# Joint last stage: PSUM dealt out as two banks for jobs and two for the turned probabilities, instead of three and one

## What is computed

```python
xn = layernorm(x)
qkv = xn @ w_qkv.T                       # 16 heads of 16 columns
q, k = rmsnorm(q) * q_norm_w, rmsnorm(k) * k_norm_w
p = softmax(q @ k.T * 16 ** -0.5)        # per sequence and head, 256 x 256
s = (p @ v) @ w_proj.T + b_proj
# 8 experts of width 176, two of them kept per token, and a shared expert of 352
g = sum_e c[e] * (silu(xn @ gate[e]) * (xn @ up[e]) @ down[e]) + shared(xn)
x = x + s * silu(g)
```

## Time and profile before

| | |
|---|---|
| median of 3 runs | 1460.88 us (1456.83 to 1460.98) |
| the profiled execution: device time | 1457.64 us |
| its span | 1455.8 us |
| mean granted clock of TensorE | 0.98 |
| PE busy over the span | 1374.6 us, 94% |
| DVE, ACT, POOL busy | 63%, 56%, 53% |
| the last stage | from 909.5 us to the end, 546 us |

### The profile page before, as it was taken

How to read it: one execution, slowest core, us unless ns; L and a number is a source line. 1 busy time by engine, 2 the same in 40 slices (tenths; PEclk the granted TensorE clock), 3 DMA queues, 4 the chain that set the end, 5 groups by cost and what they waited for, 6 DMA issues and landing times. The chain is left out here.

```text
span 1455.8 us, 25701 instructions
## 1 busy us (share of the span) xinstructions
PE 1374.6 (94%) x8880; PEld 1231.8 (85%) x8880; DVE 917.8 (63%) x1781; ACT 822.4 (56%) x2172; POOL 764.7 (53%) x759
## 2 busy tenths in 40 slices
PE   6988799999999999999999997889999999999997
PEld 5877689998899989998899986678888888889896
DVE  5554565665656565666656664676777777776654
ACT  4543454445444554445554443367777687777773
POOL 1642243445344454435455434577669667766764
PEclk9999999999999999999999999899999999999999
DMA  5877333234331343323433423234233232342442
GB/s 171 292 265 263 82 93 99 74 83 115 111 87 48 106 123 100 89 52 102 124 87 79 118 80 130 78 122 128 81 103 118 85 118 90 107 131 85 127 132 72
DMA packets 85681, 165.64 MB, mean 114 GB/s; under 512 B 16720, under 2 KB 27664, under 8 KB 83248
## 3 DMA queue, kind: packets, MB, share of 16 engines
q1 hardware_dynamic: 85552, 163.99, 37.2%
HBM read 99.90 MB, written 22.09 MB: 84 GB/s over the span
## 5 line engine op out<-in xcount | busy, mean ns | idle before, releaser
L750 POOL TENSOR_TENSOR a_pr<-a_pr,a_ri 128x512 f32<-128x512 f32 x128 | 133.2, 1041 | 304.7 <-DVE a_ri L930 304.5
L807 ACT ACTIVATE a_pr<-a_score,a_nb 128x256 f32<-128x256 f32 x256 | 118.9, 469 | 270.2 <-DVE a_nb L922 270.2
L1277 POOL TENSOR_TENSOR l_pr<-l_pr,l_ri 128x512 f32<-128x512 f32 x128 | 133.2, 1041 | 136.5 <-DVE l_ri L1647 135.3
L1405 ACT ACTIVATE l_pr<-l_score,l_nb 128x256 f32<-128x256 f32 x256 | 119.1, 471 | 84.1 <-DVE l_nb L1618 83.4
L55 PE MATMUL a_job<-s_xs,s_wh 128*128 128x512 f32 x384 | 156.1, 407 | 5.1 <-PEq L204 5.1
L56 PE MATMUL a_job<-s_xs,s_wh 128*128 128x512 f32 x384 | 152.6, 397 | 0.0
L57 PE MATMUL a_job<-s_xs,s_wl 128*128 128x512 f32 x384 | 151.9, 396 | 0.0
L922 DVE TENSOR_REDUCE a_nb<-a_score 128x2 f32<-128x512 f32 x128 | 88.4, 691 | 89.7 <-PE a_score L993 89.4
L1618 DVE TENSOR_REDUCE l_nb<-l_score 128x2 f32<-128x512 f32 x128 | 87.4, 683 | 29.4 <-PE l_score L1743 29.1
L935 DVE TENSOR_TENSOR a_pt<-a_turn,a_pt 128x512 fp32r<-128x512 f32 x128 | 87.4, 683 | 24.4 <-ACT a_pt L815 24.4
L1767 PE MATMUL l_out<-s_wh,l_vp 128*128 128x256 f32 x512 | 93.1, 304 | 0.9 <-DVE s_wh L1622 0.9
(11 more groups left out here) (239 smaller groups left out, 4811.5 us busy)
## 6 DMA issues: line engine op xcount, KB each, us to landing
s_wl<-wgu_scratch SPq DMA_DIRECT2D x56, 512.0 KB, 4.7
a_sk<-a_rotk SPq DMA_DIRECT2D x384, 64.0 KB, 2.0
a_sq<-a_rotq SPq DMA_DIRECT2D x256, 64.0 KB, 2.0
s_xs<-xn_scratch SPq DMA_DIRECT2D x14, 1024.0 KB, 5.7
l_wd<-wd_scratch SPq DMA_DIRECT2D x56, 256.0 KB, 2.7
a_raw<-in_w SPq DMA_DIRECT2D x30, 256.0 KB, 3.0
wgu_scratch<-f_split SPq DMA_DIRECT2D x14, 512.0 KB, 4.5
f_praw<-in_moe_w SPq DMA_DIRECT2D x14, 384.0 KB, 3.5
```

The lines of the kernel that those rows point to most:

```text
L750: pool.tensor_tensor(e, e, ri[:, n % 2, :].unsqueeze(2).broadcast_to([P, 2, SEQ]), ALU.mult)\
L807: i = act.activation(pr[:, n % 2, t, :], PS[n % 2][:, t * SEQ:(t + 1) * SEQ], ACT.Exp, bias=nb[:, n % 2, t:t + 1], accum_out=sm[:, n % 2, ...
L1277: pool.tensor_tensor(e, e, ri[:, n % 3, :].unsqueeze(2).broadcast_to([P, 2, SEQ]), ALU.mult)\
L1405: i = act.activation(pr[:, n % 3, t, :], PS[n % NPS][:, t * SEQ:(t + 1) * SEQ], ACT.Exp, bias=nb[:, n % 3, t:t + 1], accum_out=sm[:, n % 3 ...
```

## The change

The job banks become two instead of three, and `turn` becomes two banks, used by even and odd units. `turn(n)` then waits for the low part of unit n - 2 and no longer for that of n - 1. No instruction is added, removed or put in another place on any engine; the banks and the semaphores that are waited for differ. The total stays at eight banks.

```diff
-    NJ, NPS, NSTK, NGU, ND, NCB, NHID = 3, 1, 3, 3, 3, 3, 3
+    NJ, NPS, NSTK, NGU, ND, NCB, NHID = 2, 1, 3, 3, 3, 3, 3
@@
         PJ = [n_.ps(f"job{i}") for i in range(NJ)]
         PS = [n_.ps(f"score{i}") for i in range(NPS)]
-        PT = n_.ps("turn")
+        PT = [n_.ps(f"turn{i}") for i in range(2)]
@@ ACT, turn_hi
-                    act.activation(pt[:, n % 2, 0, :], PT[:, :], ACT.Copy).then_inc(S["turn_hi"], 1)
+                    act.activation(pt[:, n % 2, 0, :], PT[n % 2][:, :], ACT.Copy).then_inc(S["turn_hi"], 1)
@@ DVE
-                        dve.tensor_tensor(pt[:, n % 2, 1, :], PT[:, :], pt[:, n % 2, 0, :], ALU.subtract).then_inc(S["turn_free"], 1)
+                        dve.tensor_tensor(pt[:, n % 2, 1, :], PT[n % 2][:, :], pt[:, n % 2, 0, :], ALU.subtract).then_inc(S["turn_free"], 1)
@@ PE
                 def turn(n):
                     pe.wait_ge(S["norm_ready"], n + 1)
-                    if n >= 1:
-                        pe.wait_ge(S["turn_free"], n)
+                    if n >= 2:
+                        pe.wait_ge(S["turn_free"], n - 1)
                     for kc in range(2):
                         for t in range(2):
-                            i = pe.transpose(PT[:, kc * SEQ + t * P:kc * SEQ + (t + 1) * P], pr[:, n % 3, t, kc * P:(kc + 1) * P],
+                            i = pe.transpose(PT[n % 2][:, kc * SEQ + t * P:kc * SEQ + (t + 1) * P], pr[:, n % 3, t, kc * P:(kc + 1) * P],
                                              ident[:, :])
```

## The result

The changed kernel took 1471.7 us (median of 4 runs, 1469.72 to 1480.06), the kernel before in the same comparison 1458.86 (4 runs): +12.8 us. The ratio is 1.0106, 95% interval [1.0078, 1.0134]. The profiled execution took 1469.72 us with a span of 1467.9, 12.1 more than before. The forecast was 1473, from a sum of +12.5.

The account below looks back on a forecast made before the run. PE's own instruction list was taken to bound the last stage. 24.8 - 4.1 - 7.7 - 2 + 1.5 = +12.5 us on the profiled 1457.6 gave 1470.1, plus 3.2 to the median 1473.3, said as 1473; range 1463 to 1489.

Parts of the forecast that it names:

- PE's list bounds the stage: Last stage: PE's own instruction list sets the time, so the change is worth the idle it removes or adds there.
- Term one, the turn bank: Idle ahead of 31 turns, 13.6 us, cut at 0.38 each by the second turn bank: -7.7 us, ceiling 9.3.
- Term two, the job bank: With two job banks 40 of 232 jobs start late, 24.8 us, less 4.1 of waits PE already has.
- The sign that was named: Profile after: PE waits for job banks some 20 us in all, the largest near 950, 1075 and 1135.
- What the turns absorb: Bank stalls just before turns shorten the 5.9 us of idle left there: between 0 and 5.9, taken as 2.
- The clock, +1.5: New long idles on PE bring none to two more falls to half clock, 0 to 3.1 us; one taken, +1.5.
- Faster: Rival: the second turn bank saves all 13.6 us ahead of turns and bank stalls are swallowed; 1454 us, 6 in 100.
- The cascade through the score bank: Rival: delayed G's product on DVE holds up maximum, exponentials and next scores, +6.9 us; 1480, up to 1489; 14 in 100.
- The clock did not swing: Rival judged here: each of 18 groups of late jobs takes a clock fall of 1.5, another +25 us, 1498; 4 in 100.
- The upper end: Nothing saved at turns and both long stalls costing a clock fall: +23.8 us, with a rival added up to 28.
- the values' wait: Sign: in the profile after, values on PE newly wait for DVE's low part, 3 to 6 us.
- PE's share of the stage: Sign: PE's busy share of the last stage 2 points lower in the profile after.

Follow-up runs that it names:

- e5: Control: the kernel before (three job banks, one turn bank) with its two down banks made one, so output is not the reference's; 1458.04 us, ratio 1.0011.
- e6: Three job banks and two turn banks, one down bank as in the control e5, output not the reference's; 1450.34 us, ratio to the kernel before 0.9955.
- e8: Two job banks and two turn banks, one down bank as in the control e5; 1472.25 us, ratio to the kernel before 1.0110.
- e1: The kernel before with two job banks instead of three, still one turn bank, one bank unused; 1475.79 us against 1459.75, ratio 1.0118.
- e7: Four job banks and one turn bank, one down bank as in the control e5; 1456.94 us, ratio to the kernel before 1.0004.
- e11: The kernel before with DVE's low part of unit n - 2 put ahead of its maximum of unit n + 1; 1507.51 us, ratio 1.0348.
- e9: The changed kernel with DVE's copy of a Q job ahead of ACT's square, which reads the copy; 1479.00 us, ratio to the kernel before 1.0164.

## Why the prediction was right

- **PE's list bounds the stage.** Held: same work, and the whole 12.6 us are in the distances between PE's starts.
- **Term one, the turn bank, -7.7 (at most 9.3).** Measured alone: -7.7 (e5 to e6). The rule behind it, that a turn gives back only up to the values behind it, shows in the trace: idle moves from L1753 to L1767. The agreement in the number has luck in it. I cut at 0.38 with 0.15 from release to start, where the values in the place shown start after 0.06, and I did not see the 0.16 of each wait that the view hides. Beside two job banks, which is the kernel at hand, the measured gain is about 3 and not told apart from nothing.
- **Term two, the job bank, +24.8 less 4.1 = +20.7.** Measured: +22.5 in the jobs' distances, +21.9 in time with two turn banks (e6 to e8), +16.0 with one (e1). Laying each job against the release of the bank two before, in a trace where nothing waited for it, gave the size to a tenth beside two turn banks; the 16.0 with one stands 4.7 under it and has in it what the turns absorb. With three banks the wait binds in two places only, the 3.2 us of Q1 for Q0, and e7, which takes these away, is no faster beyond the noise. The sign that was named, some 20 us of bank waits, came with 22.1. One sentence beside the term reads the trace wrongly: of the twelve large late jobs, six found a Q in their bank, one a T, but four a G and one a U; there is no P or C among them. The sum does not use it. The large stalls are where they were placed: 3.83, 2.63 and 2.78 of idle at G4, G17 and U23, for 4.69, 2.50 and 3.02 late.
- **What the turns absorb, -2 of 5.9.** Turn side in all: -18.8 + 7.2 + 1.4 = -10.2, forecast -9.7. More directly, the idle ahead of values is 8.2 us with three job banks (e6) and 5.6 with two (e8): 2.6 taken by the stalls. By time, the turn bank gives some 3 instead of 7.7 beside two job banks, so this part was reckoned too small if anything; term two's smaller size in e1 may be the same overlap.
- **The clock, +1.5.** Wrong in its net. Both forecast falls came, behind the stalls at G17 and U23:

```profile
1082.70:1085.90 3.20, 3.20 (x10) 2.52 (x11) 0.00 (x0) 0.69 (x2) 2.19 (x2) 0.50 0.20 83
1147.50:1150.80 3.30, 3.30 (x14) 2.99 (x13) 1.50 (x3) 0.68 (x2) 1.28 (x1) 0.50 0.02 5
```

  Besides, the fall behind G4's stall lasts 6.8 us instead of 3.4, which the prediction had not counted, and one near 1035 is new. But falls of before near 1152, 1210, 1275 and 1350 us are gone, and from its first to its last matmul the stage has 33.0 us at 0.50 after and 33.1 before. On these two traces the term should have been zero; that the total is still right to 0.3 us has luck in it.
- **Rivals.** "Faster" needed bank stalls under 9 us net, and they are 16 to 22. The cascade through the score bank is in the trace with +1.4 us, where 6.9 was its price. The clock did not swing with the small idles: 32 bank waits, 18 of them under 0.4 us, left the time at 0.50 where it was. The upper end, "up to 28" with "the second rival", does not add up: it means the cascade, the third in the list, and 23.8 + 6.9 is 30.7.

Of the other signs, the values' wait (3 to 6 us; 3.2 for L1622, 5.6 in all) came. PE's share of the stage fell by 1 point and not by 2 (507.5 us busy of 546.3 before, 513.0 of 558.4 after); the stretch shown above is the one that fell most. DVE's idle ahead of L1526 grew from 45.1 to 52.1 us, but that ahead of L1618 did not (29.4 to 27.8).

## What to carry to other kernels

To price a buffer taken away, lay every use against the release of the one N - 1 places before, in the trace that has N: the lateness, less waits that already stand behind for the same releaser, came near the cost here (20.7 for 16 to 22). To price one added, ask what the next instruction on the same engine waits for: if it is the same event, the gain is capped by the length of what can slip in front. And before moving a step out of a late reader's way, follow the reader's other inputs and the step's new neighbours: here each single move lost or gained nothing. At G17 two paths of like length led to the same copy, and in e11 the step brought its own wait along.

## What the runs showed that was not expected

- A matmul's row outlasts the next start by 0.16 us (0.39 against 0.23 for 128x512), so 31 waits ahead of turns, shown with 13.6 us, were worth 18.1 when they vanished.
- Half clock also came without any idle in front: in the kernel before from 1151.9 us, after a stretch in which PE was busy all the time, mostly with matmuls of 8 columns (L). What made the clock fall there, no run tells. Such falls came and went between the traces, and e9's trace has 13.5 us more of half clock than the changed kernel's.

```profile
1148.00:1151.80 3.80, 3.80 (x36) 3.80 (x36) 0.89 (x5) 2.08 (x8) 3.25 (x10) 1.00 0.03 6
1151.90:1155.20 3.30, 3.30 (x17) 3.30 (x17) 2.40 (x9) 1.65 (x6) 0.12 (x1) 0.50 0.01 2
```
- The low part in front of the maximum cost 50 us over 128 units (e11), though the scores had shown one wait of 1.5 us before. The margins told how tight the round was (a quarter of the scores started under 0.72 us behind the exponentials), and the step's own wait, 48.7 us for ACT, told that it was more than its 0.6 us.
